# Keys projected straight into the turned layout, their norms summed by ones in column tiles, and all stage lists rewritten

## The reference

```python
q, k, v = x_n @ w_q, x_n @ w_kv[:, :1024], x_n @ w_kv[:, 1024:]      # 16 heads of 64
q = q / max(|q|, 1e-12) * q_scale                                    # per row and head
k = k / max(|k|, 1e-12) * k_scale
scores = 8 * q @ k.T - slope[h] * distance, causal, null keys in front
out = softmax(scores) @ v @ w_out
```

## Time and profile before

| | |
|---|---|
| median of 3 runs | 1038.4 us (1037.4 to 1041.18) |
| the profiled execution's own time | 1040.48 us |
| its span, from first to last instruction | 1038.8 us |
| mean granted TensorE clock | 0.973 of full speed |
| PE busy | 959.0 us, 92% |
| DVE busy | 784.6 us, 76% |
| ACT busy | 613.4 us, 59% |
| POOL busy | 583.8 us, 56% |

### The profile page before, as it was taken

How to read it: one execution, slowest core, us unless ns; L and a number is a source line. 1 busy time by engine, 2 the same in 40 slices (tenths; PEclk the granted TensorE clock), 3 DMA queues, 4 the chain that set the end, 5 groups by cost and what they waited for, 6 DMA issues and landing times. The chain is left out here.

```text
span 1038.8 us, 22173 instructions
## 1 busy us (share of the span) xinstructions
PE 959.0 (92%) x8405; PEld 740.9 (71%) x8405; DVE 784.6 (76%) x2393; ACT 613.4 (59%) x1288; POOL 583.8 (56%) x570
## 2 busy tenths in 40 slices
PE   0888899999999999999999999999999999999976
PEld 0566778687676868677686868778686777768755
DVE  6877678879788787879788796887788776873575
ACT  4417773876558653876538663785537674686621
POOL 4227563765558463764647573665638554664641
PEclk9968899999999999999999999999999999999998
DMA  6300000000000000000000000000000000000000
GB/s 159 90 0 1 11 2 2 1 11 1 13 1 1 12 12 2 1 11 3 12 2 1 11 12 1 1 11 2 12 1 1 1 13 2 1 1 2 12 1 11
DMA packets 22091, 11.53 MB, mean 11 GB/s; under 512 B 7648, under 2 KB 21344, under 8 KB 21856
## 3 DMA queue, kind: packets, MB, share of 16 engines
q1 hardware_dynamic: 18272, 8.86, 3.2%
q10 hardware_dynamic: 3712, 1.25, 0.5%
HBM read 8.00 MB, written 2.10 MB: 10 GB/s over the span
## 5 line engine op out<-in xcount | busy, mean ns | idle before, releaser
L871 POOL TENSOR_TENSOR rnorm<-sumsq,minus_half 128x16 f32<-128x16 f32 x64 | 186.7, 2936 | 15.4 <-DVE sumsq L1490 14.1
L879 POOL TENSOR_TENSOR unit<-unit,causal 128x256 f32<-128x256 f32 x128 | 93.2, 750 | 95.7 <-ACT unit L1121 95.7
L879 POOL TENSOR_TENSOR square<-square,causal 128x256 f32<-128x256 f32 x128 | 97.6, 785 | 69.1 <-ACT square L1121 68.6
L1890 PE MATMUL bank<-qT,kT 64*128 64x256 f32 x512 | 95.2, 389 | 0.0
L1115 ACT ACTIVATE square<-bank,bias_k,rnorm 128x256 f32<-128x256 f32 x128 | 65.6, 569 | 38.6 <-PE bank L1890 38.6
L1484 DVE TENSOR_REDUCE sumsq<-square 128x16 f32<-128x1024 f32 x64 | 77.9, 1217 | 13.7 <-ACT square L1068 12.9
L1896 PE MATMUL bank<-qT,kT 64*128 64x128 f32 x512 | 84.0, 284 | 2.3 <-ACT unit L1121 1.5
L1061 ACT ACTIVATE unit<-bank 128x512 f32<-128x512 f32 x128 | 72.4, 602 | 20.1 <-PE bank L1664 17.8
L1896 PEld LDWEIGHTS bank<-qT,kT 64*128 64x128 f32 x512 | 71.0, 186 | 17.7 <-issue 6.1
L1669 PEld LDWEIGHTS bank<-ident,unit 128*128 128x128 f32 x520 | 60.6, 143 | 24.1 <-DVE unit L1496 11.1
L1669 PE MATMUL bank<-ident,unit 128*128 128x128 f32 x520 | 69.8, 279 | 7.1 <-DVE unit L1496 5.7
(11 more groups left out here) (385 smaller groups left out, 2755.6 us busy)
## 6 DMA issues: line engine op xcount, KB each, us to landing
xin<-in_L_attn_x SPq DMA_DIRECT2D x7, 256.0 KB, 2.8
out<-x SPq DMA_DIRECT2D x7, 256.0 KB, 2.3
square<-in_L_attn_w_kv SPq DMA_DIRECT2D x1, 1024.0 KB, 8.2
w_sw<-in_L_ffn_sw_w SPq DMA_DIRECT2D x3, 256.0 KB, 6.2
unit<-in_L_attn_w_q SPq DMA_DIRECT2D x1, 512.0 KB, 6.0
w_out<-in_L_attn_w_out SPq DMA_DIRECT2D x8, 64.0 KB, 2.1
w_ml<-in_L_ffn_ml_w SPq DMA_DIRECT2D x2, 256.0 KB, 5.9
xin<-in_L_attn_x ACTq DMA_DIRECT2D x1, 256.0 KB, 3.2
```

Source lines behind the costliest of these rows:

```text
L871: pool.tensor_tensor(rnorm[:, k, t, :], sumsq[:, t % 2, k, :], minus_half[:], ALU.pow).then_inc(a_root.sem, 1)
L879: m = pool.tensor_tensor(pd, pd, causal[:].unsqueeze(1).to_broadcast([P, 2, P]), ALU.mult)
L1890: return mm(bank[s][:, 2 * P * i:2 * P * (i + 1)], kT[rs, p, 2 * P * b:2 * P * b + P], qT[rs, p, 2 * P * b:2 * P * (b + 1)], start=True, s ...
```

## The change

K is no longer projected in rows. `a_k.i` (i = 0 to 3) makes, in each of two ring uses, one product of a head pair's weights with all 512 columns of `xaT`, so that it comes out turned; ACT copies it to `kT` and also squares it out of the same bank into a K slot of `unit`, and gives the bank back after both. `a_kr.r` sums four squares at a time with a stationary of ones and zeros (`sel_k`) in four 32-column tiles of `bank[3]`, in float32; two rounds accumulate. `a_ks` copies the sums to SBUF, `a_kt` turns them, `a_kss` clamps them (DVE) and takes the root in two halves, one for each sequence (POOL). `a_m.t` makes Q alone and `a_ss.t` sums Q alone. `score_exps` waits for the half it needs. `l_turn2`, the next user of `bank[3]`, waits for `a_kss`. The increments of `dve_passed` go. All lists are rewritten; of the middle ones those of PE, DVE and POOL are shown below, and in the first group `a_m.0 a_null a_m.1 a_k.0 a_t.0` becomes `a_m.0 a_m.1 a_k.0 a_null a_k.1 a_t.0`. At the end of DVE's prologue `l_xl.0 s_bias l_xl.1 E_sum` becomes `l_xl.0 E_sum s_bias l_xl.1`.

```diff
 MIDDLE = {
     "PE": """
-f_clock a_m.0 a_m.1 a_null a_k.0 f_turn.0 f_turn.1 f_ce.0 f_ce.1 f_sw.0 a_t.0 a_m.2 f_me.0 l_turn2 f_sw.1 f_ceT
-a_v.0 f_relu.0 f_relu.1 f_sw.2 f_ce2 a_k.1 a_t.1 a_m.3 f_sw.3 a_v.1 a_k.2 f_ce2T f_me.1 a_t.2 f_ml.0 a_k.3 f_ml.1
-f_ml.2 a_t.3 f_ml.3 a_v.2 a_v.3 f_out.0 l_turn3 f_out.1 l_route a_scores.0 f_out.2 f_out.3 l_g.0 l_cT a_nT
-a_scores.1 l_u.0 a_mix.0 l_c.0 a_scores.2 l_g.1 l_u.1 a_mix.1 l_g.2 e_turn1 l_c.1 a_scores.3 l_u.2 a_mix.2 l_c.2
-a_scores.4 l_u.3 l_g.3 a_mix.3 a_scores.5 l_g.4 a_mix.4 a_scores.6 l_u.4 a_mix.5 l_c.3 a_scores.7 a_mix.6 l_down.0
+f_clock a_m.0 a_m.1 a_null f_turn.0 a_k.0 f_turn.1 f_ce.0 f_ce.1 a_k.1 f_sw.0 f_me.0 a_kr.0 a_t.0 a_m.2 a_k.2 f_ceT
+f_sw.1 a_k.3 f_relu.0 f_relu.1 f_sw.2 f_ce2 a_t.1 a_m.3 a_kr.1 f_sw.3 a_kt f_me.1 l_turn2 a_v.0 a_t.2 a_v.1 f_ce2T
+f_ml.0 f_ml.1 a_t.3 a_v.2 f_ml.2 f_ml.3 a_v.3 l_turn3 f_out.0 f_out.1 l_route a_scores.0 a_nT l_g.0 f_out.2 f_out.3
+l_g.1 l_cT a_scores.1 l_u.0 a_mix.0 a_scores.2 a_mix.1 e_turn1 l_c.0 a_scores.3 l_u.1 l_g.2 a_mix.2 l_c.1 a_scores.4
+l_g.3 l_u.2 a_mix.3 l_c.2 a_scores.5 l_u.3 l_g.4 a_mix.4 l_c.3 a_scores.6 l_u.4 a_mix.5 a_scores.7 a_mix.6 l_down.0
...
     "DVE": """
...
-a_nexp l_res f_pick l_norm l_turn3 l_route l_pick l_coef f_out.0 f_out.1 f_out.2 f_out.3 f_end_stats a_nT l_cT
-e_stats l_hg.0 l_hu.0 a_mix.0 e_apply l_hc.0 l_hg.1 a_mix.1 l_hu.1 l_hc.1 e_scan l_hg.2 l_hu.2 a_mix.2 f_end a_mix.3
-l_hg.3 l_hu.3 l_hc.2 a_mix.4 a_mix.5 l_hg.4 l_hc.3 e_sum l_hu.4 a_mix.6 l_dstats.0 a_mix.7 l_end.0 l_dstats.1
+f_stats.0 f_stats.1 f_apply.0 f_apply.1 a_ss.0 a_null f_route f_ce a_u.0 f_hid.0 a_ss.1 f_ce_apply a_ss.2 f_hid.1
+a_u.1 a_u.2 f_hid.2 f_ce2 a_ss.3 a_kss f_hid.3 l_turn2 f_ce2_apply a_u.3 l_res f_pick l_norm l_turn3 a_nexp f_out.0
+l_route e_stats l_pick f_out.1 a_nT l_hg.0 l_coef f_out.2 f_out.3 a_mix.0 l_cT e_apply l_hg.1 a_mix.1 l_hu.0 l_hc.0
+e_scan l_hg.2 l_hu.1 a_mix.2 l_hc.1 l_hu.2 f_end_stats l_hg.3 a_mix.3 e_sum l_hc.2 l_hu.3 a_mix.4 f_end l_hc.3
+a_mix.5 l_hg.4 l_hu.4 a_mix.6 l_dstats.0 a_mix.7 l_end.0 l_dstats.1 l_astats.0 l_end.1 l_astats.1 a_o.0 l_aapply.0
...
     "POOL": """
...
-l_turn2 l_res f_bias a_scores.0 a_scores.1 e_stats a_scores.2 f_end_stats a_scores.3 a_keep e_scan a_scores.4
+a_keep f_stats.0 f_stats.1 a_ss.0 f_ce a_ss.1 a_ss.2 f_ce_apply f_ce2 a_ss.3 l_turn2 a_kss.0 l_res f_bias e_stats
+a_kss.1 a_scores.0 a_scores.1 a_scores.2 a_scores.3 e_scan a_scores.4 a_scores.5 f_end_stats a_scores.6 a_scores.7
...
+        k_square = [unit[:, i // 2, i % 2, :] for i in range(4)]
+        k_sums = k_square[0]
+        k_sumsq = k_square[1][:, 0:T * H].rearrange("p (t h) -> p t h", h=H)
...
-            def norms(g, t, k):
+            def k_norms(g, b):
+                pool.wait_ge(a_kss.sem, a_kss.at(g))
+                ts = slice(2 * b, 2 * b + 2)
+                pool.tensor_tensor(rnorm[:, 0, ts, :], k_sumsq[:, ts, :], minus_half[:].unsqueeze(1).to_broadcast([P, 2, H]),
+                                   ALU.pow).then_inc(a_kroot.sem, 1)
...
-            def flat_k(g, t):
+            def flat_k(g, i):
                 for k in range(2):
-                    n = use("k", t, k)
+                    n = use("k", i, k)
+                    r, c = k_round(i, k)
                     act.wait_ge(a_put.sem, a_put.at(g, n + 1))
-                    act.activation(kT[:, 4 * k:4 * k + 4, t * P:(t + 1) * P], bank[n % 3][:].rearrange("p (c n) -> p c n", n=P),
-                                   ACT.Copy).then_inc(a_took.sem, 1)
+                    act.activation(kT[:, k_pair(i, k), :], bank[n % 3][:], ACT.Copy)
+                    if r:
+                        act.wait_ge(a_ksum.sem, a_ksum.at(g, 1))
+                    act.activation(k_square[c], bank[n % 3][:], ACT.Square).then_inc(a_took.sem, 1)
...
                 dve.wait_ge(s.sem, s.at(g, 4))
-                dve.sem_inc(dve_passed, 1)
                 for t in range(T):
...
-            def a_k(g, t):
+            def a_k(g, i):
...
+                    mm3(bank[n % 3][:], w_kv[:, p * P:(p + 1) * P], xaT).then_inc(a_put.sem, 1)
+
+            def a_kr(g, r):
+                if r == 0:
+                    pe.wait_ge(a_nullc.sem, a_nullc.at(g, 1))
+                pe.wait_ge(a_took.sem, a_took.at(g, use("k", 2 * r + 1, 1) + 1))
+                for c in range(4):
+                    last = mm(bank[3][32 * c:32 * c + 32, :], sel_k[:, r, :], k_square[c], start=(r == 0), stop=(r == 1),
+                              skip_group_check=True)
+                last.then_inc(a_ksum.sem, 1)
+
+            def a_kt(g):
+                pe.wait_ge(a_kcol.sem, a_kcol.at(g))
+                turn(bank[3], lambda t: k_sums[:, t * P:(t + 1) * P]).then_inc(a_kturn.sem, 1)
```

More of the change, by code:

```diff
@@ L59 @@
     "PE": """
[L60 to L63, removed]
+a_m.0 a_m.1 a_k.0 a_null a_k.1 a_t.0 a_m.2 a_k.2 a_kr.0 a_k.3 a_t.1 a_kr.1 a_m.3 a_kt l_turn2 a_v.0 a_t.2 a_v.1
@@ L64 @@
+a_t.3 l_turn3 a_v.2 l_route l_g.0 l_u.0 a_v.3 l_g.1 a_nT a_scores.0 l_u.1 l_cT l_g.2 l_u.2 a_scores.1 l_c.0 a_mix.0
+a_scores.2 a_mix.1 e_turn1 a_scores.3 l_g.3 a_mix.2 a_scores.4 l_g.4 a_mix.3 l_c.1 a_scores.5 l_c.2 a_mix.4 l_c.3
+a_scores.6 l_u.3 a_mix.5 a_scores.7 l_u.4 a_mix.6 l_down.0 l_down.1 a_mix.7 l_down.2 l_down.3 a_out.0 a_out.1 l_x.0
+l_x.1
 """,
     "DVE": """
-a_ss.0.0 a_ss.0.1 a_ss.1.0 a_null a_u.0 a_ss.1.1 l_turn2 a_ss.2.0 a_u.1 a_ss.2.1 l_res a_ss.3.0 l_norm a_ss.3.1
-a_u.2 l_turn3 a_u.3 a_nexp l_hg.0 l_route l_pick e_stats l_coef l_hg.1 l_hu.0 l_hu.1 a_nT l_hg.2 a_mix.0 l_hu.2 l_cT
@@ L115 @@
     "PE": """
-f_clock a_m.0 a_m.1 a_null f_turn.0 f_turn.1 a_k.0 f_sw.0 f_ce.0 f_ce.1 a_t.0 a_m.2 f_sw.1 f_me.0 a_v.0 f_ceT
-l_turn2 f_sw.2 f_relu.0 f_relu.1 a_k.1 f_ce2 a_t.1 a_m.3 f_sw.3 a_v.1 a_k.2 f_me.1 a_t.2 f_ce2T a_k.3 f_ml.0 f_ml.1
-f_ml.2 f_ml.3 a_t.3 a_v.2 f_out.0 l_turn3 a_v.3 f_out.1 f_out.2 l_route l_g.0 a_scores.0 a_nT f_out.3 l_cT l_g.1
-a_scores.1 l_u.0 a_mix.0 l_c.0 a_scores.2 l_u.1 a_mix.1 a_scores.3 l_g.2 a_mix.2 a_scores.4 l_u.2 a_mix.3 l_c.1
-a_scores.5 l_c.2 l_g.3 a_mix.4 l_u.3 l_g.4 l_c.3 a_scores.6 l_u.4 a_mix.5 a_scores.7 l_down.0 a_mix.6 l_down.1
@@ L121 @@
-a_mix.7 l_down.2 l_down.3 a_out.0 a_out.1 l_x.0 l_x.1
+f_clock a_m.0 a_null a_m.1 a_k.0 f_turn.0 f_turn.1 f_sw.0 a_k.1 f_ce.0 f_ce.1 f_sw.1 a_kr.0 f_me.0 a_t.0 a_m.2 f_ceT
+f_sw.2 f_relu.0 f_relu.1 a_k.2 a_k.3 f_ce2 a_t.1 a_m.3 f_me.1 f_sw.3 a_kr.1 a_v.0 a_kt f_ml.0 l_turn2 f_ml.1 f_ml.2
+a_t.2 f_ml.3 f_ce2T a_v.1 f_out.0 f_out.1 a_t.3 l_turn3 a_v.2 a_v.3 l_route f_out.2 a_nT a_scores.0 f_out.3 l_g.0
+l_cT l_u.0 a_scores.1 l_g.1 a_mix.0 l_c.0 a_scores.2 l_u.1 a_mix.1 l_c.1 a_scores.3 l_g.2 a_mix.2 a_scores.4 l_u.2
@@ L122 @@
+l_g.3 a_mix.3 a_scores.5 l_u.3 l_g.4 a_mix.4 l_c.2 a_scores.6 l_u.4 a_mix.5 l_c.3 a_scores.7 a_mix.6 l_down.0
+l_down.1 a_mix.7 l_down.2 l_down.3 a_out.0 a_out.1 l_x.0 l_x.1
 """,
     "DVE": """
-f_stats.0 f_stats.1 a_ss.0.0 f_apply.0 a_ss.0.1 f_apply.1 a_null a_ss.1.0 a_ss.1.1 a_u.0 f_hid.0 f_route f_ce a_u.1
-f_ce_apply f_hid.1 a_ss.2.0 f_hid.2 a_ss.2.1 f_ce2 l_turn2 a_u.2 a_ss.3.0 a_ss.3.1 f_ce2_apply f_hid.3 a_u.3 l_res
-f_pick l_norm a_nexp l_turn3 f_out.0 f_out.1 l_route l_pick f_out.2 l_coef l_hg.0 f_out.3 a_nT f_end_stats l_hg.1
@@ L127 @@
-l_cT a_mix.0 l_hu.0 f_end l_hu.1 a_mix.1 l_hc.0 a_mix.2 a_mix.3 l_hc.1 l_hg.2 l_hu.2 l_hc.2 l_hg.3 a_mix.4 l_hu.3
-l_hc.3 l_hg.4 l_hu.4 a_mix.5 a_mix.6 l_dstats.0 a_mix.7 l_end.0 l_dstats.1 l_astats.0 l_end.1 l_astats.1 a_o.0
-l_aapply.0 l_aapply.1 a_end.0 a_o.1 l_xl.0 l_xl.1 a_end.1
+f_stats.0 f_stats.1 a_ss.0 f_apply.0 f_apply.1 a_u.0 f_hid.0 a_null f_ce f_route f_ce_apply f_hid.1 a_ss.1 f_hid.2
+a_u.1 a_ss.2 f_ce2 a_u.2 f_ce2_apply f_hid.3 a_ss.3 a_kss f_pick l_turn2 l_res a_u.3 a_nexp l_norm l_turn3 l_route
@@ L141 @@
+l_dstats.0 l_astats.0 l_dstats.1 a_o.0 l_astats.1 a_o.1
 """,
```

239 lines of the change are left out of this document (128 added, 111 removed).

## The result

| | before | after |
|---|---|---|
| median | 1037.9 us (1037.05 to 1041.18) | 989.3 us (987.93 to 989.75) |
| profiled execution, its span | 1040.48, 1038.8 us | 989.75, 988.0 us |
| granted TensorE clock | 0.973 | 0.981 |

The ratio is 0.9522 (95% interval 0.9499 to 0.9544). Run again later, the changed kernel gave 988.3 us and 0.9506 (0.9491 to 0.9522).

The account below looks back on a forecast made before the run. PE, busy 92% of the span, was taken as the bound. Terms -7.4 (PE work), -10.5 (stall), -1.5 (first group) and -1 (fronts) gave -20.4 on 1040.5, 1020.1; with the median 2.1 lower, 1018 us, range 1002 to 1038.

Parts of the forecast that it names:

- So a round lies between 0.86 (overlap) and 3.44 (none); I take 0.86: PE's `a_kr` rounds: tiles overlap fully, 0.86 us each, within PE's term of -0.93 us per group, -7.4 over 8.
- The estimate of 1.09 for a round: Alternative for `a_kr` on PE, with the skill's tile efficiency of 0.79: this term -3.7 us instead of -7.4.
- Between 0 and all of the 21 us come back; I take half: PE's stall at `l_hg` in five groups, 4.2 us each: moving `f_end` behind `a_mix.4` brings -10.5 us.
- This lies beside PE's work and pays only through shorter stalls: DVE loses 7.4 of 95 us per group, 1.8 from 18 removed increments; no term of its own in the sum.
- The sign of 725 us of busy time on DVE: Sign in the profile after: DVE busy near 725 us in all.
- The front orders of all groups together: -1: Reordered fronts of all groups: -1 us, bounds -8 (idle time of the middle groups) and +16 (K bank waits).
- `a_kss.1`... no margin: Rival, chance 0.11, slower: key roots on POOL come too late for the mask `a_mix.0` needs; above 1050 us.
- ACT takes the gain back: Rival, chance 0.11: K banks held 1.1 us against 0.7 make PE wait 2 to 3 us a group; 1036 us.
- The stall only moves: Rival, chance 0.20: `f_end` costs the same behind `a_mix.4` and PE drops to half clock there too; 1029 us.
- All of it goes: Rival, chance 0.12: DVE with 7 us less to do no longer holds anything up; 1004 us.
- First group, -1.5: First group: `a_t.0` starts about 2.9 us earlier, but `a_k.0` needs both halves of `xaT`; net -1.5, between -4 and +2.
- The last part, 0 (bounds -3 and +3): Prologue and last part, reordered with the same work: 0 us, bounds -3 and +3.

Follow-up runs that it names:

- e11: Changed kernel with the first round of `a_kr` made three times, two more rounds a group: 1003.0 us, ratio 0.968.
- e3: Kernel before with `f_end` alone moved behind `a_mix.4` in DVE's middle list: 1017.3 us, ratio 0.977.
- e15: Kernel before, order untouched, GpSimd's causal masks cut from 128 to 4 columns (only its time means anything): 1017.8 us, ratio 0.9794.
- e4: Changed kernel with all 18 unread increments per group put back on DVE: 997.5 us, ratio 0.9589.
- e9: New way to make the keys, increments left out, every other stage in the order of the kernel before: 1060.3 us, ratio 1.0203.
- e1: Kernel before, with its old keys and increments, played with the changed kernel's new lists: 1069.2 us, ratio 1.028.
- e0: Changed kernel run again, unaltered: 988.3 us.
- e7: Changed kernel with its middle lists behind `l_route` in the order of the kernel before: 1010.3 us, ratio 0.9746.
- e8: Kernel before with the second half of its middle groups in the changed kernel's order: 1037.4 us, ratio 0.9991.
- e2: Changed kernel with `f_end_stats` and `f_end` back at their early places in the middle lists: 995.8 us, ratio 0.9578.
- e6: Changed kernel with the lists of the last group's last part (`LAST_F`) in the order of before: 992.6 us.
- e5: Kernel before with the unread increments on VectorE left out, nothing else changed: 1030.5 us, ratio 0.9914.

## Why the prediction was right or wrong

- **"So a round lies between 0.86 (overlap) and 3.44 (none); I take 0.86": right.** 0.855 (e11). Added up from start to next start, the 64 transposes of 7.25 us in a middle group became 36 of 3.72 us, and the two rounds with their switches cost 1.99: -1.5 us a group where the sum had -0.93. The estimate of 1.09 for a round, from the Trainium skill ("TensorE: Matmul & The Clock Gate", Part 3), would have made the two added rounds of e11 2.2 us a group; 1.7 were measured.
- **"Between 0 and all of the 21 us come back; I take half": the step that failed first.** The cause of the stall was read rightly. All of it came back (e3, e15). The walk through the new order charged `f_end` 2.7 to 4.3 us behind `a_mix.4`, its duration at the old place. I had written that POOL's work beside it probably slowed it, and did not ask what POOL does at the new place. It rests there, and `f_end` costs 1.8. In the middle groups of e3 this gave 18.8 us, where 10.5 were booked. (The 21 was itself 2 too high: the clock fell in four groups of five, so 5 x 2.5 + 4 x 1.7 = 19.3.) In the changed kernel `f_end` even waits for its own root on POOL, and POOL's next mask begins at 491.23, when the four are done:

```profile
489.78 1.12 DVE L1338 TENSOR_SCALAR x4m<-x4m,n_f_mv,n_f_rstd 128x128 f32<-128x128 f32 x4 [0.67 <-POOL n_f_rstd L860]
```

- **"This lies beside PE's work and pays only through shorter stalls" (the increments): wrong.** The sum had them at nothing; they cost 7 to 9 us in the changed kernel (e4). The 0.1 us for one was right in size: 18 of them would be 1.8 us in a chain, and a group grew by 1.3. But DVE's busy share says nothing of the short chains at the group's seam, for which PE waits with nothing else to do. The sign of 725 us of busy time on DVE came out at 738 for a like reason: the profile counts no increment as busy (e4 has them, and its seven groups show 592.4 us against 592.2), yet the sign had 1.8 us a group taken off for them.
- **"The front orders of all groups together: -1": the second large miss.** A front got 3.0 us shorter in a middle group, and the same in the last attention (51.9 to 48.9). 1.5 are PE's own work and 1.1 what the increments cost in this front (e4); some 0.4 is left to the order. The idle time of this front was only 1.15 us before, so part of it stood in the busy time: with the increments back the same instructions of PE in this front are busy for 51.58 us instead of 51.24 (e4). My lower bound of -8 for all fronts counted idle time alone.
- **"`a_kss.1`... no margin", "ACT takes the gain back", "The stall only moves": none of the three came.** In the middle groups `a_mix.0` waits for no mask, no K bank wait is in the front, and the clock stays at 1.00 in the mixing part. But the slower side was near: with the order not made for it the new keys' front is 1.4 us longer than the old one (e9), with the keys not made for it the order's is 4.7 longer (e1). "All of it goes" (0.12) was the mechanism that held, and its 1004 was still 15 us too slow, because it took the front and the ends as they were.
- **First group, -1.5: no gain is seen, and the sign isn't settled.** PE's wait ahead of `a_t.0` fell from 3.94 us to 0.58, as the steps said. But DVE makes the second half of `xaT` at 84.6 us instead of 80.4 in the two traces of the result, so the work begins later. Both ends of this stretch vary between runs whose lists are the same up to there. The first half of `xaT` comes at 77.9 (e0), 78.2 (e7) and 80.6 us (after) with the new prologue, at 74.9 (e3, e8) and 76.0 (before) with the old: 2 to 6 us later. The first middle group starts at 173.9 to 177.2 us in six runs with the new lists (after, e0, e2, e6, e7, e11) and at 172.0, 172.0 and 176.1 with the old (e3, e8, before).
- **The last part, 0 (bounds -3 and +3): wrong.** -5.0, of which 4.3 are its order (e6). I had read no row of it: its wait of 2.7 us for `ce_rows` and a clock of 0.90 stood in the trace.

Per middle group the 7.6 us are: 4.1 for the stall (2.5 of waiting, 1.6 of clock), 1.5 of PE's own work, 1.4 for the increments, and 0.6 for the rest, which I put down to the order. This split takes the increments at their price in the changed kernel and the stall at its price in the kernel before; taken the other way round they are 0.6 (e5) and 1.7 to 4.3 (e2, e7), and the difference belongs to keys and order together. Added up over the span, of the 30 us that the sum lacks about 8 are the stall, 8 the increments, 5 PE's own work (1.5 instead of 0.93 in eight groups) and 4 the order of the last part; the rest lies in the orders of the other groups, less the first group's 2. What is not settled is how the 5.1 and 4.5 us of the last two groups split; only their fronts were compared.

## What to carry to other kernels

A duration read at one place holds for that place: before you charge it elsewhere, look what the other engines do there, above all GpSimd beside VectorE. Where the bounding engine is busy for 92%, ask of each stage also which short chain at the seams it stands in; work "beside" the bound is free only where something covers it. And an order written by hand fits the work that it was written for: halves of such a change, tried alone, can both lose.
